# The last part of a four-part transformer kernel: masked keys in place of masked queries, score tiles of 32 rows, three sequences in flight, and keys and values made during the scan

## The chip, the core and the metric

The kernel runs on one core of a Trainium2 chip. Its engines are TensorE (PE in the profile; PEld is its weight load), VectorE (DVE), ScalarE (ACT), GpSimd (POOL) and SyncE (SP, which here only issues transfers). TensorE writes into PSUM, eight banks of 512 float32 per partition; DVE and ACT read PSUM, POOL cannot. The metric is the device time of one launch, in microseconds.

## What is computed

Four attention blocks follow each other on 16 sequences of 256 tokens of width 256. This change touches the end of the third block (a recurrence over the tokens, the scan) and the whole of the fourth:

```python
# third block, its end
def step(s, u_t):
    s = jax.nn.silu(s @ A.T) + u_t
    return (s, s)
_, states = jax.lax.scan(step, jnp.zeros((builder_state.shape[0], S), U.dtype), U.transpose(1, 0, 2))
ssm_out = jnp.einsum('tbs,sh->bth', states, Cmat)
x = residual + ssm_out
# fourth block: dec is x, enc is a context of 77 tokens, 16 heads of 16
q = (dec @ Wq).reshape(b, dec_len, NUM_HEADS, D_HEAD)
kv = enc @ Wkv
kk, v = jnp.split(kv, 2, axis=-1)
attn = jnp.einsum('bihd,bjhd->bijh', q, kk) / jnp.sqrt(jnp.float32(D_HEAD))
attn = jax.nn.softmax(attn, axis=1)
out = jnp.einsum('bijh,bjhd->bihd', attn, v).reshape(b, dec_len, D_INNER)
y = dec + out @ Wfc + bfc
mu = jnp.mean(y, axis=-1, keepdims=True)
var = jnp.mean(jnp.square(y - mu), axis=-1, keepdims=True)
return (y - mu) / jnp.sqrt(var + LN_EPS) * gamma + beta
```

The state has 64 elements per sequence. The softmax of the fourth block runs over the 256 tokens (axis 1), so with the 77 context tokens on the partitions it is a reduction along a row. All matrix products are float32; each such matmul shows as two records in the trace, for every count below.

## The kernel before

The main part (the first two blocks and the third up to the input of the scan, three sequences in flight) is the same in both kernels. Behind it come three stretches.

**Set-up of the scan.** SP issues four transfers: the mean's input, the scan's input `S` (`drive`), the weights of the last part and three rows of parameters. POOL clears some tiles. TensorE then multiplies the input of all tokens (L1670), 32 tokens of all 16 sequences per PSUM bank, eight matmuls of 512 columns into the eight banks. ScalarE waits for all eight.

**The scan.** 254 steps: TensorE multiplies the last state (16 columns) and adds it to its place in PSUM (L1676), ScalarE applies SiLU (L1688), and so on in turn. Nothing else runs. Both engines run it as a loop of two steps with register arithmetic.

**The last part.** For each of 16 sequences `b`: `state` (POOL adds the state and the input, L1762), `dec` (TensorE, L1841, then DVE adds the residual, L1902), `decb` (POOL, L1769), `turn` (four transposes, L1851, evacuated by ACT, L1995), `queries` (L1821, evacuated by ACT, L2004), `keys` (L1821 with 77 columns, ACT L1975) and `values` (L1832, ACT L1987) from a context tile that SP loads (L1747). Then the heads. A score matmul contracts over all 128 partitions, which hold 8 heads of 16, so the other heads must be zero in one operand: POOL's `spread` (L1785) multiplies the queries by a mask, one instruction of 128x256 per head, 16 per sequence. A unit is two heads: one matmul of 512 columns (L1862), DVE's maxima (L1908), ACT's two exponentials with their sums (L2017), DVE's reciprocal of the sums (L1916) and the values scaled by it (L1924). Eight units per sequence. `weigh` (L1872) multiplies weights and values in four 32-column tiles at once, `outputs` (L2026) evacuates, `out` (L1881) projects, then residual (L1933), moments (L1939 to L1945), `rstd` (POOL, L1791), normalise (L1955), gamma and beta (POOL, L1797 and L1802), and the store.

Buffers of the last part exist twice (`TWO = 2`, indexed by `b % TWO`), and so do the statistics of a unit. The order of all steps on each engine is made when the program is built: `plan3()` lists the steps with a cost each and what they wait for, `Plan.order()` lays them out by these costs, and every engine then runs its list strictly in order. A PSUM bank is taken by that plan too. A helper in the main part (L1131) puts matmuls without use into gaps of TensorE; it is not used in the scan or the last part.

## Time and profile before

| | us |
|---|---|
| median of 3 runs | 3063.52 |
| lowest and highest | 3044.8, 3069.33 |
| the profiled execution | 3032.12, span 3030.4 |
| main part, up to 2477 us of the span | 2477.0 |
| set-up of the scan, to 2500.5 | 23.5 |
| scan, to 2730.6 | 230.1 |
| last part, to 3030.4 | 299.8 |

### The profile page before, as it was taken

What the parts mean: (1) busy time and instruction counts of PE and PEld (TensorE: products, weight loads), DVE (VectorE), ACT (ScalarE), POOL (GpSimd) and SP (SyncE); (2) the same over time, 40 slices, a digit from 0 to 9 for tenths busy, and PEclk for the clock granted to TensorE, in tenths of its full rate; (3) what the DMA queues carried; (4) which work ended last, traced back from release to release, by engine and by line L of the source; (5) the groups of instructions that cost most, each with busy time, mean ns of one, the idle gap of its engine ahead of it and who ended that gap; (6) DMA issues with size and microseconds to landing.
All of it is one profiled execution on the core that took longest, in us unless ns stands there. A gap on an engine that the chain in (4) does not pass through costs nothing. (4 is left out here: it accounts for less than half of the span.)

```text
span 3030.4 us, 50406 instructions
## 1 busy us (share of the span) xinstructions
PE 2663.9 (88%) x18092; PEld 1968.6 (65%) x18092; DVE 1787.2 (59%) x4271; ACT 1388.1 (46%) x3588; POOL 878.0 (29%) x1096
## 2 busy tenths in 40 slices
PE   5799999999999999999999999999999974449997
PEld 4577676767676767677777777777767653335443
DVE  3975667666667676667576667575764320005776
ACT  2545455445454554555454454445453312225554
POOL 3540223323232232322232323232321010006676
PEclk9899999999999999999999899999999995559999
DMA  4230101111111111111111111111110010001110
GB/s 190 57 54 3 24 20 34 29 24 34 21 34 27 30 27 27 27 26 28 26 27 26 27 27 30 23 30 23 29 24 10 6 42 0 0 0 38 37 33 23
DMA packets 222419, 90.65 MB, mean 30 GB/s; under 512 B 205280, under 2 KB 212784, under 8 KB 221424
## 3 DMA queue, kind: packets, MB, share of 16 engines
q1 hardware_dynamic: 215728, 67.68, 11.3%
q10 hardware_dynamic: 6464, 19.93, 1.8%
q8 instruction: 144, 2.36, 0.3%
q14 instruction: 83, 0.68, 0.1%
HBM read 27.80 MB, written 9.44 MB: 12 GB/s over the span
## 5 line engine op out<-in xcount | busy, mean ns | idle before, releaser
L1097 PE MATMUL psum<-hT,w_l 128*128 128x256 f32 x2048 | 465.6, 382 | 13.7 <-ACT hT L1433 13.6
L1097 PEld LDWEIGHTS psum<-hT,w_l 128*128 128x128 f32 x2048 | 382.7, 190 | 75.3 <-ACT hT L1433 14.9
L1131 PE MATMUL psum<-w_l 128*128 128x256 f32 x1524 | 382.4, 397 | 7.0 <-ACT work L1557 5.9
L1557 ACT ACTIVATE work<-psum,nbias,qs 128x256 f32<-128x256 f32 x512 | 281.5, 567 | 150.5 <-DVE nbias L1269 147.7
L1131 PEld LDWEIGHTS psum<-w_l 128*128 128x128 f32 x1524 | 287.8, 196 | 67.7 <-issue 18.3
L1573 ACT ACTIVATE work<-psum 128x1024 f32<-128x1024 f32 (+1 forms) x224 | 220.7, 1021 | 241.4 <-PE psum L1029 215.8
L817 POOL TENSOR_TENSOR rstd<-ms,half 128x2 f32<-128x2 f32 (+1 forms) x144 | 101.2, 704 | 629.3 <-DVE ms L1190 483.2
L1266 DVE TENSOR_REDUCE nmax<-psum 128x4 f32<-128x1024 f32 (+1 forms) x192 | 206.5, 1076 | 69.9 <-PE psum L977 69.7
L857 POOL TENSOR_SCALAR work<-work 128x1024 f32<-128x1024 f32 x128 | 136.0, 1062 | 369.2 <-DVE work L1363 345.8
L922 PE MATMUL psum<-hT,w_l 128*128 128x256 f32 x896 | 214.9, 386 | 28.1 <-ACT hT L1433 27.3
L1109 PE MATMUL psum<-w_l,work 128*128 128x256 f32 x1024 | 227.5, 380 | 10.1 <-ACT hT L1433 6.9
L1109 PEld LDWEIGHTS psum<-w_l,work 128*128 128x128 f32 x1024 | 193.3, 190 | 39.7 <-DVE work L1394 12.8
L1676 PE MATMUL psum<-w_l,a_pad 128*64 x508 | 99.3, 275 | 130.6 <-ACT w_l L1688 130.6
L922 PEld LDWEIGHTS psum<-hT,w_l 128*128 128x128 f32 x896 | 163.9, 190 | 62.7 <-issue 25.9
L1285 DVE TENSOR_REDUCE nmp<-psum 128x4 f32<-128x1024 f32 x128 | 148.1, 1218 | 59.6 <-PE psum L991 59.6
L1433 ACT ACTIVATE hT<-psum,cols 128x256 f32<-128x256 f32 x256 | 121.4, 528 | 130.2 <-PE psum L913 129.3
L1363 DVE TENSOR_SCALAR work<-work,rsum 128x256 f32<-128x256 f32 x512 | 176.4, 408 | 4.5
L1676 PEld LDWEIGHTS psum<-w_l,a_pad 128*64 128x64 f32 x508 | 73.4, 206 | 158.0 <-issue 158.0
L931 PE MATMUL psum<-w_l,xhat 128*128 128x256 f32 x640 | 162.3, 398 | 12.6 <-DVE xhat L1342 8.6
L1902 DVE TENSOR_TENSOR w_l<-w_l,psum 128x512 f32<-128x512 f32 x16 | 10.9, 683 | 256.5 <-PE psum L1841 256.4
L2017 ACT ACTIVATE work<-psum,nmax 77x256 f32<-77x256 f32 x256 | 117.6, 464 | 87.8 <-DVE nmax L1908 82.5
L931 PEld LDWEIGHTS psum<-w_l,xhat 128*128 128x128 f32 x640 | 121.7, 197 | 46.0 <-DVE xhat L1342 14.8
(187 smaller groups left out, 4844.2 us busy)
## 6 DMA issues: line engine op xcount, KB each, us to landing
w_l<-in_w_l ACTq DMA_DIRECT2D x1, 5120.0 KB, 25.6
x_res<-in_x SPq DMA_DIRECT2D x16, 256.0 KB, 2.7
res<-x_res ACTq DMA_DIRECT2D x16, 256.0 KB, 3.3
w_l<-res SPq DMA_DIRECT2D x16, 256.0 KB, 2.8
out<-w_l ACTq DMA_DIRECT2D x16, 256.0 KB, 2.0
w_l<-in_w_l ACTq DMA_DIRECT2D x1, 3072.0 KB, 14.0
work<-work SPq DMA_TRANSPOSE x192, 3.1
w_l<-in_w_l SPq DMA_DIRECT2D x2, 1024.0 KB, 8.4
```

Source lines behind the costliest of these rows:

```text
L857: eng.tensor_scalar(e, e, 1.0, MAGIC, ALU.mult, ALU.add).then_inc(*even.next((a.name, u, i, p)))
L922: mm = eng.matmul(banks.tile(key)[:, ft * n:(ft + 1) * n], wt[:, k, ft * P:(ft + 1) * P], src(k), start=(k == 0), stop=(k == KT - 1))
L931: mm = eng.matmul(banks.tile(key)[0:n, m * D:(m + 1) * D], src(k, m), wt[:, k, :], start=(k == 0), stop=(k == KT - 1))
L1097: mm = eng.matmul(banks.tile(key)[:, h * TOKENS:(h + 1) * TOKENS], w1[:, k, h, m * P:(m + 1) * P], hT[p][:, k, :], start=(k == 0), stop=(k ...
L1109: mm = eng.matmul(banks.tile(key)[:, tt * D:(tt + 1) * D], actT(p)[:, m, tt * P:(tt + 1) * P], w2[:, m, :], start=(m == 0), stop=(m == MT ...
L1131: eng.matmul(psum[:, bank, 0:TOKENS], w[0][:, 0:P], w[0][:, 0:TOKENS], start=True, stop=True)
L1266: eng.tensor_reduce(m, s, X, ALU.max, negate=True).then_inc(*norm_step.next(("max", a.name, u, i, p)))
L1285: eng.tensor_reduce(nmp[p][:, half, tile, 64 * i:64 * i + 64:16], s.rearrange("p r (j n) -> p (r j) n", j=2), X, ALU.max, negate=True).the ...
L1363: ins = eng.tensor_scalar(e, e, rsum[:, r, h:h + 1], 255.0, ALU.mult, ALU.min)
L1557: ins = eng.activation(e[:, h * TOKENS:(h + 1) * TOKENS], s[:, h, :], ACT.Exp, bias=nbias[:, r, h:h + 1], scale=qs[:, ATTENTIONS.index(a), ...
L1573: eng.activation(pt(n, p)[0:a.kp, :], banks.pair(key)[0:a.kp, :, :].rearrange("p r n -> p (r n)"), ACT.Exp) \
L1676: eng.matmul(z[0:STATE, n, :], a_pad[:, 0:STATE], G[:, :, n], start=False, stop=True, skip_group_check=True).then_inc(ag_done, 1)
```

## The change

- **Keys are masked, not queries.** For each sequence there are two copies of the keys, one with the even and one with the odd heads kept (`par` is the mask's column, 1 or 0 per partition). A block of 32 partitions holds two heads; a score matmul takes 32 rows of one of the copies, in which one of the two is zero, and the plain queries. POOL's `spread` is gone. A unit is now four heads (`i` picks 64 of the 128 partitions): four matmuls of 32 rows and 256 columns into a pair of banks, two row blocks side by side; one DVE maxima over 77x1024; four exponentials; one reciprocal of four sums; one scaling of 64 elements. Four units per sequence.
- **Three sequences in flight** (`LATE = 3`), three of each buffer, two statistics slots for each.
- **Keys and values are made during the scan.** All 16 context tiles are loaded in the set-up. From step 64 on, every 11 steps, four pieces stand behind a step's matmul: two of the keys (two matmuls of 77 columns each) and two of the values (one of 256 columns). DVE evacuates them in three instructions per sequence.
- **Behind each other step stands a matmul without use** of 208 columns. The scan is written out, without a loop. The eighth input matmul is done before step 33, and ScalarE starts after the first.
- `turn` is evacuated by DVE instead of ACT. The values are scaled as 16 columns per head, with zeros around them, in place of 32. The plan's costs changed, and with them the order.

```diff
-TWO = 2
+LATE = 3
...
+UNITS3 = [(ft, i) for ft in range(KT) for i in range(2)]
...
-        k = add("tensor", "keys", 0, 1.0, *loads, fills=[(("k", b), "scalar", "keys", 0)])
-        v = add("tensor", "values", 0, 0.9, k, fills=[(("v", b), "scalar", "values", 0)])
...
-        slots = [add("pool", "spread", u, 0.9, q, earlier(b, "tensor", "scores", None, 4 + u)) for u in range(4)]
...
+        for u, (ft, i) in enumerate(UNITS3):
+            x = add("tensor", "scores", u, 0.5, q, fills=[(("s", u, b), "scalar", "exps", u)])
+            before = scaled[u - HELD] if u >= HELD else earlier(b, "vector", "scale", None, last)
+            x = add("vector", "maxima", u, 1.25, x, before)
+            x = add("scalar", "exps", u, 2.25, x, earlier(b, "tensor", "weigh", None, ft))
+            scaled.append(add("vector", "scale", u, 0.45, x, *scaled[-1:], earlier(b, "tensor", "weigh", None, ft)))
+            if i:
+                x = add("tensor", "weigh", ft, 0.95, scaled[-1], fills=[(("o", ft, b), "scalar", "outputs", ft)])
+                o.append(add("scalar", "outputs", ft, 0.5, x, earlier(b, "tensor", "out", None, 0)))
...
+        BESIDE = 208
+        BEGIN, EVERY = 2 * CHUNK, 11
...
+                for b in range(BATCH):
+                    eng.dma_start(ctx3[b].rearrange("p k c -> p (k c)"), t["ctxT"][b]).then_inc(kv_in, 16)
...
-                for p in range(TWO):
-                    eng.memset(vpad[p][:, 0, :, :], 0.0).then_inc(blank, 1)
-                eng.wait_ge(blank, TWO)
+                for p in range(LATE):
+                    eng.memset(vs[p], 0.0).then_inc(blank, 1)
+                eng.wait_ge(blank, LATE)
...
+                for b in range(BATCH):
+                    eng.wait_ge(kv_full, b + 1)
+                    for j in range(2):
+                        eng.tensor_scalar(kx3[b][:, j, :, :].rearrange("p f n -> p (f n)"), psum[:, 1, 0:KT * CTX], par[:, j:j + 1], None, ALU.mult)
+                    eng.tensor_copy(v3[b][0:CTX, :], psum[0:CTX, 1, D:2 * D]).then_inc(kv_taken, 1)
...
-                for c in range(TOKENS // CHUNK):
+                last = TOKENS // CHUNK - 1
+                def preload(c):
                     eng.matmul(psum[:, c, :], a_pad[:, :], S[:, :, c * CHUNK:(c + 1) * CHUNK].rearrange("p b t -> p t b"),
                                start=True, stop=True).then_inc(au_done, 1)
+                for c in range(last):
+                    preload(c)
                 eng.wait_ge(zeroed, 2)
...
-                with eng.Fori(0, (TOKENS - 2) // 2) as i:
-                    step(2 * i + 1)
-                    step(2 * i + 2)
+                def idle(bank):
+                    eng.matmul(psum[:, bank, 0:BESIDE], beside[:, 0:P], beside[:, 0:BESIDE], start=True, stop=True)
+                def keys_of(b, ft):
+                    if not b and not ft:
+                        eng.wait_ge(kv_in, 16 * BATCH)
+                        eng.wait_ge(late_in, 32)
+                    if b and not ft:
+                        eng.wait_ge(kv_taken, b)
+                    for k in range(KT):
+                        eng.matmul(psum[:, 1, ft * CTX:(ft + 1) * CTX], wk3[:, k, ft * P:(ft + 1) * P], ctx3[b][:, k, :],
+                                   start=(k == 0), stop=(k == KT - 1))
+                def values_of(b, k):
+                    mm = eng.matmul(psum[0:CTX, 1, D:2 * D], ctx3[b][:, k, :], wv3[:, k, :], start=(k == 0), stop=(k == KT - 1))
+                    if k == KT - 1:
+                        mm.then_inc(kv_full, 1)
+                for n in range(1, TOKENS - 1):
+                    if n == CHUNK + 1:
+                        preload(last)
+                    step(n)
+                    b, piece = divmod(n - BEGIN, EVERY)
+                    if n < BEGIN or b >= BATCH or piece >= 2 * KT:
+                        idle(0 if n > CHUNK else last)
+                    elif piece < KT:
+                        keys_of(b, piece)
+                    else:
+                        values_of(b, piece - KT)
...
-                eng.wait_ge(au_done, TOKENS // CHUNK)
+                eng.wait_ge(au_done, 1)
...
-                with eng.Fori(0, (TOKENS - 2) // 2) as i:
-                    eng.wait_ge(ag_done, 2 * i + 1)
-                    step(2 * i + 1)
-                    eng.wait_ge(ag_done, 2 * i + 2)
-                    step(2 * i + 2)
+                for n in range(1, TOKENS - 1):
+                    eng.wait_ge(ag_done, n)
+                    step(n)
...
-                    for h in (2 * g, 2 * g + 1):
-                        eng.tensor_scalar(kbd3(b)[:, h, :], qT3(b)[:, ft, :], mask16[:, h:h + 1], 1.0, ALU.mult,
-                                          ALU.mult).then_inc(*qbd_ready.next((ft, b, h)))
...
-                    ft, g = units3[u]
+                    ft, i = UNITS3[u]
                     key = ("s", u, b)
-                    ready(key, (qbd_ready, (ft, b, 2 * g + 1)), *([] if u else [(k3_ready, b)]))
-                    eng.matmul(banks3.tile(key)[0:CTX, :], kT3(b)[:, ft, :], kbd3(b)[:, 2 * g:2 * g + 2, :],
-                               start=True, stop=True).then_inc(*banks3.filled(key))
+                    ready(key, *([] if u else [(q3_ready, (b, KT - 1))]))
+                    for j in range(2):
+                        for r in range(2):
+                            g = slice(64 * i + 32 * r, 64 * i + 32 * r + 32)
+                            mm = eng.matmul(banks3.pair(key)[0:CTX, r, j * TOKENS:(j + 1) * TOKENS], kx3[b][g, j, ft, :],
+                                            qT3(b)[g, ft, :], start=True, stop=True)
+                    mm.then_inc(*banks3.filled(key))
...
-                            mm = eng.matmul(banks3.tile(key)[32 * c:32 * c + 32, 0:TOKENS], vs[b][0:CTX, n, :],
+                            mm = eng.matmul(banks3.tile(key)[32 * c:32 * c + 32, 0:TOKENS], vs[b][0:CTX, n, 16 - 16 * h:48 - 16 * h],
                                             pt3(b)[0:CTX, n, :], start=(h == 0), stop=(h == 1))
...
+                def turn(_, n, b):
+                    key = ("decT", b)
+                    eng.wait_ge(*banks3.at(key))
+                    if b >= LATE:
+                        eng.wait_ge(*banks3.at(("q", b - LATE)))
+                    eng.tensor_copy(hT[b % LATE][:, :, :].rearrange("p a b -> p (a b)"), banks3.tile(key)) \
+                        .then_inc(*banks3.released(key, decT_ready, b))
...
-                    key, r = ("s", u, b), b % TWO * TWO + u % TWO
+                    key, r = ("s", u, b), slot3(u, b)
                     eng.wait_ge(*banks3.at(key))
-                    eng.tensor_reduce(nmax[0:CTX, r, 0:2], banks3.tile(key)[0:CTX, :].rearrange("p (h n) -> p h n", h=2),
+                    eng.tensor_reduce(nmax[0:CTX, r, 0:4], banks3.pair(key)[0:CTX].rearrange("p r (j n) -> p (r j) n", j=2),
                                       X, ALU.max, negate=True).then_inc(*max3_ready.next((u, b)))
...
-                    eng.reciprocal(rsum[0:CTX, r, 0:2], sums[0:CTX, r, 0:2]).then_inc(*den3.next((u, b)))
+                    eng.reciprocal(rsum[0:CTX, r, 0:4], sums[0:CTX, r, 0:4]).then_inc(*den3.next((u, b)))
...
-                    eng.tensor_tensor(vs[b][0:CTX, h:h + 2, :], vpad[b % TWO][0:CTX, 0, h:h + 2, :],
-                                      bcast(rsum[0:CTX, r, 0:2].unsqueeze(2), [CTX, 2, 32]), ALU.mult) \
+                    eng.tensor_tensor(vs[b][0:CTX, h:h + 4, 16:32], v3[b][0:CTX, h * 16:h * 16 + 64].rearrange("p (h d) -> p h d", h=4),
+                                      bcast(rsum[0:CTX, r, 0:4].unsqueeze(2), [CTX, 4, 16]), ALU.mult) \
...
-                    for h in range(2):
-                        eng.activation(pt3(b)[0:CTX, ft * 8 + 2 * g + h, :], s_[:, h, :], ACT.Exp,
-                                       bias=nmax[0:CTX, r, h:h + 1], accum_out=sums[0:CTX, r, h:h + 1]) \
-                            .then_inc(*banks3.released(key, exp3_done, (u, b, h)))
+                    s_ = banks3.pair(key)[0:CTX].rearrange("p r (j n) -> p (r j) n", j=2)
+                    for n in range(4):
+                        ins = eng.activation(pt3(b)[0:CTX, h + n, :], s_[:, n, :], ACT.Exp,
+                                             bias=nmax[0:CTX, r, n:n + 1], accum_out=sums[0:CTX, r, n:n + 1])
+                    ins.then_inc(*banks3.released(key, exp3_done, (u, b)))
...
```

What the engines run in the two places that matter, as the program lists it. TensorE from the set-up to the end of the scan, before (w_l is the large tile that holds input and states, a_pad the step's weights; two steps per turn of the loop):

```order
L1670 MATMUL psum<-w_l,a_pad 128x512 x8
L1679 UNCONDITIONAL_BRANCH
L1679 ISA
L1676 ISA
L1676 MATMUL psum<-w_l,a_pad 64x16
```

and in the changed kernel around step 64, where the first sequence's keys and values are made (L1729 is the step, L1734 the matmul without use, L1743 the keys, L1747 the values):

```order
L1729 MATMUL psum<-w_l,a_pad 64x16
L1734 MATMUL psum<-w_l 128x208
L1729 MATMUL psum<-w_l,a_pad 64x16
L1743 MATMUL psum<-w_l 128x77 x2
L1729 MATMUL psum<-w_l,a_pad 64x16
L1743 MATMUL psum<-w_l 128x77 x2
L1729 MATMUL psum<-w_l,a_pad 64x16
L1747 MATMUL psum<-w_l 77x256
L1729 MATMUL psum<-w_l,a_pad 64x16
L1747 MATMUL psum<-w_l 77x256
L1729 MATMUL psum<-w_l,a_pad 64x16
L1734 MATMUL psum<-w_l 128x208
```

So each step's matmul now has one other piece of work behind it in TensorE's queue.

TensorE in the middle of the last part, before (L1841 dec, L1821 keys or queries, L1832 values, L1851 turn, L1872 weigh, L1881 out, L1862 scores):

```order
L1841 MATMUL psum<-cw,w_l 128x256 x2
L1821 MATMUL psum<-w_l 128x77 x4
L1832 MATMUL psum<-w_l 77x256 x2
L1851 MATMUL psum<-ident,w_l 128x128 x4
L1872 MATMUL psum<-work,w_l 32x256 x8
L1821 MATMUL psum<-hT,w_l 128x256 x4
L1881 MATMUL psum<-w_l,xhat 128x256 x4
L1841 MATMUL psum<-cw,w_l 128x256 x2
L1862 MATMUL psum<-work,kcx 77x512 x4
```

and in the changed kernel (L1870 turn, L1895 weigh, L1884 scores, L1904 out, L1851 queries, L1860 dec):

```order
L1870 MATMUL psum<-ident,w_l 128x128 x4
L1895 MATMUL psum<-work,w_l 32x256 x8
L1884 MATMUL psum<-x_res,w_l 77x256 x8
L1904 MATMUL psum<-w_l,xhat 128x256 x4
L1884 MATMUL psum<-x_res,w_l 77x256 x4
L1851 MATMUL psum<-hT,w_l 128x256 x4
L1884 MATMUL psum<-x_res,w_l 77x256 x4
L1860 MATMUL psum<-cw,w_l 128x256 x2
L1884 MATMUL psum<-x_res,w_l 77x256 x4
```

Keys and values are gone, and score units, now four matmuls each, stand singly between steps that use the whole array.

DVE in the same stretch of the changed kernel (L1939 maxima, L1947 and L1953 the scaling, L1925 dec, L1962 residual, then the moments):

```order
L1939 TENSOR_REDUCE nmax<-psum 77x4
L1947 RECIPROCAL rsum<-sums 77x4
L1953 TENSOR_TENSOR w_l<-work,rsum 77x4x16
L1939 TENSOR_REDUCE nmax<-psum 77x4
L1925 TENSOR_TENSOR w_l<-w_l,psum 128x512
L1962 TENSOR_TENSOR w_l<-w_l,psum 128x512
L1968 BN_STATS st<-w_l 128x6 x2
```

Maxima and scalings alternate as before, with half as many of each.

## Rows read from the trace of the kernel before

**Rows 1.** Stretches by stage: us, busy us of PE, PEld, DVE, ACT, POOL, clock, DMA.
```profile
2477.00:2500.50 23.50, 14.12 (x16) 3.66 (x16) 3.97 (x4) 1.32 (x2) 4.50 (x3) 0.74 0.46 120
2500.50:2730.60 230.10, 99.28 (x508) 73.42 (x508) 0.00 (x0) 48.54 (x255) 0.00 (x0) 0.51 0.00 0
2730.60:3030.40 299.80, 266.19 (x1344) 138.92 (x1344) 197.06 (x528) 163.23 (x642) 202.91 (x336) 0.97 0.11 33
```

**Rows 2.** Timeline in the scan: start us, us, engine, line, operation, idle before.
```profile
2501.27 0.19 ACT L1688 ACTIVATE w_l<-psum  x1 [0.62 <-PE psum L1676]
2501.63 0.28 PE L1676 MATMUL psum<-w_l,a_pad 128*64 x2 [0.52 <-ACT w_l L1688]
2502.07 0.19 ACT L1688 ACTIVATE w_l<-psum  x1 [0.61 <-PE psum L1676]
...
2599.87 0.19 ACT L1688 ACTIVATE w_l<-psum  x1 [0.72 <-PE psum L1676]
2600.23 0.39 PE L1676 MATMUL psum<-w_l,a_pad 128*64 x2 [0.52 <-ACT w_l L1688]
2600.78 0.19 ACT L1688 ACTIVATE w_l<-psum  x1 [0.71 <-PE psum L1676]
```

**Rows 3.** Timeline of the main part's end: tiles and whole-array matmuls in turn.
```profile
2386.52 0.70 PE L1131 MATMUL psum<-w_l 128*128 128x256 f32 x2
...
2407.15 1.09 PE L1029 MATMUL psum<-work,kcx 32*77 32x256 f32 x8 [0.54 <-DVE work L1307]
2408.17 1.07 PE L1074 MATMUL psum<-work,vpad 77*32 77x256 f32 x16
2409.17 1.09 PE L1029 MATMUL psum<-work,kcx 32*77 32x256 f32 x8
2410.19 1.13 PE L1131 MATMUL psum<-w_l 128*128 128x256 f32 x4
```

**Rows 4.** Short stretches, two in the main part; columns as in rows 1.
```profile
155.00:160.00 5.00, 3.90 (x35) 2.69 (x34) 4.86 (x11) 0.91 (x3) 3.90 (x5) 1.00 0.00 0
1690.00:1695.00 5.00, 4.48 (x40) 1.68 (x42) 2.91 (x5) 2.61 (x4) 0.00 (x0) 0.50 0.02 3
...
2732.00:2738.00 6.00, 5.08 (x16) 4.13 (x17) 0.69 (x1) 0.30 (x1) 1.49 (x3) 0.50 0.37 111
```

**Rows 5.** The last part's middle, columns as in rows 1.
```profile
2750.00:3000.00 250.00, 231.70 (x1188) 119.41 (x1190) 177.08 (x474) 144.57 (x575) 176.00 (x295) 1.00 0.11 34
```

**Rows 6.** Groups by line in the same 250 us: count, busy us, mean ns, idle before.
```profile
L1908 DVE TENSOR_REDUCE nmax<-psum 77x2 f32<-77x512 f32 x116 | 77.8, 678 | 11.4 <-PE psum L1862 11.2
```

**Rows 7.** Groups by line, the last part: operation, shapes, count, busy us, mean ns, idle.
```profile
L1785 POOL TENSOR_SCALAR work<-x_res,mask 128x256 f32<-128x256 f32 x256 | 120.7, 491 | 54.1 <-ACT x_res L2004 38.8 <-PE psum L1862 10.1 <-PE psum L1841 5.2
L2017 ACT ACTIVATE work<-psum,nmax 77x256 f32<-77x256 f32 x256 | 117.6, 464 | 87.8 <-DVE nmax L1908 82.5 <-POOL w_l L1802 3.1 <-PE psum L1862 2.0
...
L1924 DVE TENSOR_TENSOR w_l<-vpad,rsum 77x64 f32<-77x64 f32 x128 | 51.0, 399 | 7.5 <-ACT vpad L1987 2.8 <-DVE rsum L1916 0.4
L1916 DVE RECIPROCAL rsum<-sums 77x2 f32<-77x2 f32 x128 | 19.7, 154 | 19.9 <-ACT work L2017 19.4
...
L1902 DVE TENSOR_TENSOR w_l<-w_l,psum 128x512 f32<-128x512 f32 x16 | 10.9, 683 | 256.5 <-PE psum L1841 256.4
...
L1987 ACT ACTIVATE vpad<-psum 77x128 f32<-77x128 f32 x32 | 7.0, 277 | 3.5 <-PE psum L1832 3.4
L1975 ACT ACTIVATE kcx<-psum 128x154 f32<-128x154 f32 x16 | 4.7, 293 | 4.5 <-PE psum L1821 4.4
```

**Rows 8.** Line L1285 (maxima, main part): count, min/median/max ns, first and last start.
```profile
L1285 DVE TENSOR_REDUCE nmp<-psum x128: 1187/1217/1228, 225.9 to 2375.6; 128x4 f32<-128x1024 f32 x128
```

**Rows 9.** Timeline of the last part: its beginning (clock 0.50), later, and scores.
```profile
2732.92 1.96 PE L1821 MATMUL psum<-w_l 128*128 128x77 f32 x8 [2.64 <-DMA w_l<-in_ctxT]
...
2741.85 1.01 PE L1821 MATMUL psum<-w_l 128*128 128x77 f32 x8
...
3006.42 3.60 PE L1862 MATMUL psum<-work,kcx 128*77 128x512 f32 x8
```

243 lines of the change are left out of this document (94 added, 149 removed).

## The prediction

> **What bounds the kernel now.** I read the stretches by stage first [rows 1], since the change touches only what lies behind 2477 us of the span: 23.5 us of set-up, 230.1 us of scan, 299.8 us of last part.
>
> The scan is a chain of two engines with no other work. At the full clock, for its first microseconds, one step is 2502.07 - 2501.27 = 0.80 us; at 0.50 it is 2600.78 - 2599.87 = 0.91 us [rows 2]. What differs is TensorE's pair of records, 0.28 against 0.39 us. ScalarE's 0.19 us and TensorE's wait of 0.52 us for it are the same. The granted clock is 0.51 over the scan: TensorE does little, and the chip gives it 1.2 GHz.
>
> The last part is bound by TensorE. In its middle TensorE is busy 231.7 of 250 us, at clock 1.00, DVE 177.1, POOL 176.0, ACT 144.6 [rows 5]. The 116 maxima instructions that start in the middle [rows 6], 8 per sequence, are 14.5 sequences, so a sequence takes 250 / 14.5 = 17.24 us and 15.98 us of TensorE, 12.21 of DVE, 12.14 of POOL, 9.97 of ACT. The last part is then 16 x 17.24 = 275.8 us and 24.0 us for filling and emptying.
>
> **The last part, term by term.** TensorE loses the keys (8 records in 1.01 us [rows 9]; 0.97 without the overlap), the values (two pairs of 256 columns at 0.43, 0.86 [rows 3]) and the old scores: eight records, four units, in 3.60 us [rows 9], of which the last 0.17 lies under what follows, so 0.86 a unit and 6.9 us in all. It gains four units of four 32-row matmuls each. The main part has the same form, L1029 with 32 rows, 77 columns of weights and 256 moving columns, 8 records: it starts 1.02 us before the next step's matmuls, when tiles of another shape follow [rows 3]. So 4 x 1.02 = 4.1 us. A whole-array pair behind tiles takes 0.70 us from its weight load on, 0.27 of it beside the 0.43 that a further pair adds (1.13 for two pairs, the same rows), and starts only when the one before is nearly done; the order shows whole-array steps standing singly between scores, about two more such changes per sequence, 0.15 each: 0.3. TensorE: 15.98 - 0.97 - 0.86 - 6.9 + 4.1 + 0.3 = 11.65 us.
>
> DVE: maxima 4 x 1.217 ([rows 8], there on 128 partitions) for 8 x 0.678; four reciprocals and four scalings fewer, 4 x 0.154 and 4 x 0.399 (64 elements each, as before) [rows 7]; `turn` added, which I price as the other 128x512 from PSUM, 0.683. Together 12.21 - 0.55 - 0.62 - 1.60 + 0.68 = 10.1 us. ACT drops keys 0.29, values 2 x 0.28 and turn, at most about 0.6: 8.5 us. POOL drops 16 x 0.491: 4.3 us. DVE's keys and values work moves under the scan, three instructions per 11 steps, where DVE had nothing to do [rows 1].
>
> So TensorE stays the bound, but DVE is now at 10.1 of 11.65. Before, a sequence took 17.24 / 15.98 = 1.08 of TensorE's work; by that alone it would be 12.6. Three things raise it: DVE, TensorE and ACT wait for each other in strict order within each unit (maxima, four exponentials of 0.464, scaling), with DVE nearly as full as TensorE; a unit is twice as coarse; and tiles may cost clock (below). The other end is the old 17.24. I take 13.3, nearer the lower one, since three sequences in flight give each engine other work during a wait. Filling and emptying stay 24.0, less 3.0: the first keys waited 2.64 us for their transfer [rows 9], and they stand no longer ahead of `dec`. Last part: 16 x 13.3 + 21.0 = 233.8, a gain of 66.0 us.
>
> **The scan, term by term.** Is the matmul without use hidden? At full clock the step's pair lasts 0.28. A next matmul of another shape starts about 0.08 before the last one's end (2407.15 + 1.09 against 2408.17 [rows 3]). The pair of 256 columns takes 0.70; one of 208 columns loses 48/256 of 0.43 us, so 0.62. The next step could start after 0.28 - 0.08 + 0.62 - 0.08 = 0.74 us, and ScalarE lets it start only after 0.80. It is hidden with 0.06 us to spare. Values (256 columns) give 0.82, 32 times 0.02; keys, 4 records some 0.12 us apart (8 in 1.01 [rows 9]), are hidden. The cover is thin: 0.1 us more for any of this and 254 steps cost 10 us. I take 0.82 for a step: 208 us, and 22 us gained.
>
> Does the clock hold? At 155 us TensorE was busy 3.90 of 5 us and kept 1.00; at 1690 it was busy 4.48 of 5 us, with narrow tiles around it, at 0.50 [rows 4]. The new scan is busy most of the time by this count, but with short matmuls, and the key steps stream least. I expect some stretches at half clock, 5 us in all. The written-out input matmul costs in the scan what it saved ahead of it. Sixteen context transfers, 1.3 MB, go out behind the scan's input while the DMA engines are already at a share of 0.46 [rows 1]: I charge 1.5 us. POOL's larger clearing ends well before TensorE's seven input matmuls. Gain of scan and set-up: 22 - 5 - 1.5 = 15.5 us.
>
> The Trainium skill bears on this (TensorEngine Tiling (Array Packing), section Key Properties): changing the tiling mode, not only the tile, drains TensorE. The trace agrees, with the starts a mere 0.08 us before the last end. By that rule every step of the scan drains twice, 64 columns against 128, and the last part at each score unit; both are in the sums above by the rows.
>
> **Sum.** 66.0 + 15.5 = 81.5 us. On the profiled execution, 3032.1 - 81.5 = 2950.6. The median of the three runs lies 31 us above it, in parts that the change does not touch; I carry that over: 3063.5 - 81.5 = 2982.
>
> **The rivals.**
>
> *The last part comes nearer to its bound* (0.18). 12.3 us per sequence and a scan at 0.80 throughout: 82 + 25 = 107 us, 2956. For it: 1.08 was reached before. Against: no engine then had another as full beside it.
>
> *The scan gives nothing* (0.15). The thin cover fails by 0.1 us, or the clock drops at each group of key steps: the scan stays at about 230 us, 3063.5 - 66 + 1.5 = 2999. For it: the 0.06 us, and the drop at 1690 us.
>
> *The last part hardly gains* (0.08). Evacuation binds: DVE's in-order waits for four exponentials at a time hold the maxima of other sequences, and a sequence takes 16.3 us. 3063.5 - 16 x 0.94 - 3 - 15.5 = 3030. For it: the ACT waits for L1908 were 82.5 us of the last part [rows 7]. Against: that was with TensorE as the bound. The Trainium skill warns of this (the same page, section PSUM Bottleneck): tiling speeds TensorE up but not the evacuation of PSUM, which may become the bound. The rows' 10.1 us for DVE leaves room.
>
> *Slower: the clock stays at 1.2 GHz through the scan* (0.07). Then the added matmul is a cost. Its time doubles as the narrow matmuls' did, 1.96 against 1.01 us [rows 9]: 0.62 becomes about 1.05 with its fixed part, a step 0.39 - 0.08 + 1.05 - 0.08 = 1.28 us, 254 of them 325 us, 95 more than now. With the last part's gain: 3063.5 - 66 + 95 = 3093. It decides from about 0.26 us per step on (66 / 254). Against it: TensorE comes from 12 us of full work when the scan starts, at 0.99 and above in the first steps, and keeps far busier than in the old scan; at 1.05 of 1.28 us it is busier still. The Trainium skill (TensorE: Matmul & The Clock Gate, Part 1) has it that the idle state is the throttled one and activity releases it, which is on the side of a scan that recovers; how much activity these short pairs are is for the run to tell.
>
> **How the numbers follow.** The forecast has 0.52: 2982, its own range 2960 to 3000, from 12.6 to 14.3 us per sequence and 0 to 22 us from the scan. The range for 8 in 10 takes in the better last part and the lost scan and ends before the weak last part and the slow clock: 2940 to 3030. The lower end also holds a median that falls nearer to the profiled execution. About 1% (31 us) is what a measurement of this kernel can tell from no change. Faster by over 1%: forecast, first two rivals and a little of the third, 0.87. Within 1%: the rest of the third and slow clock in part of the scan, 0.07. Slower: 0.06.
>
> **What would show it.** In the changed profile: scan steps at 0.80 to 0.83 us with the granted clock at 1.00, about 208 us from first to last SiLU, with a few slices below; a step whose matmul starts right behind the useless one's end, with no wait for ScalarE, says the cover is gone. In the last part, about 234 us: TensorE busy 85 to 90% at 1.00, score units 1.0 us apart from what follows, maxima 1.2 us each, DVE busy about 10 us per sequence, POOL a third. DVE above 90% would make it the bound; a clock below 0.95 there would say that the tiles cost clock, which my 13.3 holds only in part. Set-up of 22 to 26 us. The main part unchanged. I am wrong if the scan's clock is 0.5 or the time per sequence is outside 12.3 to 14.5 us.

## The result, and the profile after

| | us |
|---|---|
| before, median of 4 runs | 3055.61 (3044.8 to 3069.33) |
| after, median of 4 runs | 2960.64 (2954.39 to 2969.67) |
| ratio | 0.9689, 95% interval 0.9636 to 0.9742 |
| the profiled execution | 2969.67, span 2967.9 |

The change makes the kernel 95 us (3.1%) faster; 82 us were forecast.

Stretches by stage, profile of the changed kernel (us, busy us of PE, PEld, DVE, ACT and POOL with counts, granted clock, DMA share, GB/s). The lines are set-up of the scan, scan, last part, and the middle of the last part. They answer to [rows 1] and [rows 5].

```profile
2502.10:2523.40 21.30, 12.36 (x15) 3.44 (x15) 4.36 (x4) 1.47 (x2) 5.60 (x4) 0.69 0.73 192
2523.40:2722.60 199.20, 199.20 (x1083) 128.83 (x1082) 15.82 (x48) 48.58 (x254) 0.00 (x0) 1.00 0.00 1
2722.60:2967.90 245.30, 207.88 (x1410) 124.66 (x1408) 171.54 (x352) 140.98 (x577) 82.60 (x80) 0.83 0.11 35
2740.00:2940.00 200.00, 179.84 (x1219) 107.34 (x1218) 148.22 (x300) 123.60 (x511) 65.04 (x62) 0.83 0.09 31
```

Set-up and scan fell from 253.6 to 220.5 us, the last part from 299.8 to 245.3. That is 33.1 + 54.5 = 87.6 us. The scan holds the full clock throughout. The last part now runs at 0.83 instead of 0.97.

The main part takes 2502.1 us here and 2477.0 in the profile of before, with the same code. It varies from execution to execution with the time spent at half clock. Over all 14 profiles of this case the last matmul of the main part starts at 2470.0 to 2503.8 us, with 109 to 212 us of half clock ahead of it, and the short ones are those with little of it. So I compare profiles by what lies **behind the main part**, from the start of that last matmul to the end of the span: 557.4 us before, 470.1 after, 87.3 us less.

Timeline in the scan, the same profile, weight loads left out (start us, us, engine, line, operation, count, idle before). First plain steps with the matmul without use (L1734), then the first steps with keys (L1743) and values (L1747). They answer to [rows 2].

```profile
2524.13 0.29 PE L1729 MATMUL psum<-w_l,a_pad 128*64 128x16 f32 x2
2524.35 0.62 PE L1734 MATMUL psum<-w_l 128*128 128x208 f32 x2
2524.46 0.19 ACT L1769 ACTIVATE w_l<-psum 64x16 f32<-64x16 f32 x1 [0.57 <-PE psum L1729]
2524.90 0.29 PE L1729 MATMUL psum<-w_l,a_pad 128*64 128x16 f32 x2
...
2573.66 0.67 PE L1743 MATMUL psum<-w_l 128*128 128x77 f32 x4
2573.76 0.19 ACT L1769 ACTIVATE w_l<-psum 64x16 f32<-64x16 f32 x1 [0.57 <-PE psum L1729]
2574.26 0.29 PE L1729 MATMUL psum<-w_l,a_pad 128*64 128x16 f32 x2
...
2575.29 0.66 PE L1747 MATMUL psum<-w_l 128*77 128x256 f32 x2
2575.40 0.19 ACT L1769 ACTIVATE w_l<-psum 64x16 f32<-64x16 f32 x1 [0.63 <-PE psum L1729]
2575.88 0.29 PE L1729 MATMUL psum<-w_l,a_pad 128*64 128x16 f32 x2
```

A plain step is 0.77 us, one with keys 0.82, one with values 0.81. ScalarE ends at 2524.46 + 0.19 = 2524.65, yet the next step's matmul starts at 2524.90, right behind the matmul without use. By the sign that the prediction named, the cover is gone.

Groups by line in the same 200 us of the last part (count, busy us, mean ns, idle before). They answer to [rows 6] and [rows 7].

```profile
L2017 ACT ACTIVATE work<-psum,nmax 77x256 f32<-77x256 f32 x228 | 104.0, 472 | 26.2 <-DVE nmax L1939 25.9
L1939 DVE TENSOR_REDUCE nmax<-psum 77x4 f32<-77x1024 f32 x57 | 68.7, 1213 | 19.1 <-PE psum L1884 19.0
```

57 maxima, four per sequence, are 14.25 sequences. A sequence takes 200 / 14.25 = 14.04 us, with 12.62 us of TensorE, 10.40 of DVE, 8.67 of ACT and 4.56 of POOL. Filling and emptying are 245.3 - 16 x 14.04 = 20.7 us.

### The profile page after: what moved, and what is told of

The parts are those of the page before. It is cut to its first block and busy times, and to the rows that moved or that the text cites. A ratio compares the mean times of both kernels' runs of the same rounds, so it can differ in the third digit from the quotient of the medians.

```text
span 2967.9 us, 49392 instructions
## 1 busy us (share of the span) xinstructions
PE 2727.7 (92%) x18728; PEld 2023.1 (68%) x18728; DVE 1779.4 (60%) x4143; ACT 1367.0 (46%) x3524; POOL 758.7 (26%) x841
## 3 DMA queue, kind: packets, MB, share of 16 engines
q1 hardware_dynamic: 215728, 67.68, 11.5%
## 5 line engine op out<-in xcount | busy, mean ns | idle before, releaser
L1127 PE MATMUL psum<-w_l 128*128 128x256 f32 x1524 | 392.6, 405 | 7.0 <-ACT work L1553 5.9
L1105 PE MATMUL psum<-w_l,work 128*128 128x256 f32 x1024 | 227.5, 380 | 10.1 <-ACT hT L1429 6.9
L1376 DVE TENSOR_TENSOR x_res<-x_res,psum 128x512 f32<-128x512 f32 x112 | 76.6, 684 | 122.9 <-PE psum L927 63.9
L857 POOL TENSOR_SCALAR work<-work 128x1024 bf16<-128x1024 f32 x128 | 134.0, 1047 | 10.6
L1586 ACT ACTIVATE work<-psum,cols 128x256 f32<-128x256 f32 x128 | 60.3, 474 | 162.8 <-PE psum L1093 162.5
```

The costliest lines, as they stand in the source:

```text
L857: eng.tensor_scalar(rounded_part(a, u, i, p), e, -MAGIC, 1.0, ALU.add, ALU.mult) \
L1105: mm = eng.matmul(banks.tile(key)[:, tt * D:(tt + 1) * D], actT(p)[:, m, tt * P:(tt + 1) * P], w2[:, m, :], start=(m == 0), stop=(m == MT ...
L1127: eng.matmul(psum[:, bank, 0:TOKENS], w[0][:, 0:P], w[0][:, 0:TOKENS], start=True, stop=True)
```

## Experiments on the scan

**The loops of the kernel before written out, nothing else** (before, ScalarE's side alike):

```diff
-                with eng.Fori(0, (TOKENS - 2) // 2) as i:
-                    step(2 * i + 1)
-                    step(2 * i + 2)
+                for n in range(1, TOKENS - 1):
+                    step(n)
```

> The kernel before with the two loops of the scan written out and nothing else changed. Theory A: the clock stays at 0.50 and a step goes from 0.91 to about 0.88 us: 5 to 10 us less. Rival B: the loop's own instructions were the whole difference between 0.91 and 0.77: some 30 us less.

Measured: 2989.5 us against 3051.5, ratio 0.9801 (0.9758 to 0.9844); 497.8 us behind the main part against 557.4. Timeline in its scan, at half clock:

```profile
2600.16 0.19 ACT L1687 ACTIVATE w_l<-psum 64x16 f32<-64x16 f32 x1 [0.48 <-PE psum L1676]
2600.40 0.29 PEld L1676 LDWEIGHTS psum<-w_l,a_pad 128*64 128x64 f32 x2 [0.39 <-ACT w_l L1687]
2600.40 0.39 PE L1676 MATMUL psum<-w_l,a_pad 128*64 128x16 f32 x2 [0.28 <-ACT w_l L1687]
2600.83 0.19 ACT L1687 ACTIVATE w_l<-psum 64x16 f32<-64x16 f32 x1 [0.48 <-PE psum L1676]
```

Its first steps are still at the full clock, 0.57 us apart:

```profile
2520.34 0.19 ACT L1687 ACTIVATE w_l<-psum 64x16 f32<-64x16 f32 x1 [0.38 <-PE psum L1676]
...
2520.91 0.19 ACT L1687 ACTIVATE w_l<-psum 64x16 f32<-64x16 f32 x1 [0.38 <-PE psum L1676]
```

A step at half clock takes 0.67 us in place of 0.91 with the clock, TensorE's pair (0.39) and ScalarE's 0.19 as they were. Both ways between the engines got shorter. From ScalarE's end to the next matmul: 2600.40 - 2600.35 = 0.05 us, before 0.17 (2600.23 - 2600.06, [rows 2]). From the matmul's start to ScalarE's: 0.43, before 0.55. So 2 x 0.12 us of each step belonged to the loop. I had named 0.03; both theories were too low, and the gain of 62 us is twice what the rival gave. The last part is as before, 299.6 us at 0.97.

The trace of before held a sign of it that I had not asked for: the groups by line over the scan, weight loads, first before and then this kernel.

```profile
L1676 PEld LDWEIGHTS psum<-w_l,a_pad 128*64 128x64 f32 x508 | 73.4, 206 | 158.0 <-issue 158.0
```

```profile
L1676 PEld LDWEIGHTS psum<-w_l,a_pad 128*64 128x64 f32 x508 | 72.3, 202 | 99.8 <-ACT w_l L1687 97.8 <-issue 2.0
```

```profile
L1676 PEldq FUSED_REGOPS  x254: 74/74/78, 2500.7 to 2729.8; - x127
L1688 ACTq FUSED_REGOPS  x254: 74/74/83, 2501.1 to 2730.3; - x127
L1679 PEldq COMPARE_BRANCH  x127: 76/208/235, 2501.8 to 2730.0; - x127
```

In the loop the wait stands in a register instruction ahead of the load, and ahead of the activation on ScalarE; written out, it stands on the load and the activation themselves. In the trace of before the load starts 0.124 us after its register instruction does, the activation 0.121 us (medians of 250 steps). Those instructions start 0.037 us behind ScalarE's end and 0.427 behind the matmul's start, where the written-out scan has the load 0.051 and the activation 0.430 behind (medians too). So the 0.12 us of each crossing come with the register instruction that holds the wait. The branch is not on the way: it comes at every second step, and steps with and without it both take 0.907 us. The Trainium skill (Runtime: NRT & Kernel Launch, Instruction fetch mechanics) warns of branches for another reason, a fetch stall, and says that kernels prefer full unrolling. The equal steps show no such stall here.

**The same with the matmul without use** (in place of nothing behind the step, with the eighth input matmul at step 33 and ScalarE starting after the first):

```diff
+                    if n == CHUNK + 1:
+                        preload(last)
                     step(n)
+                    eng.matmul(psum[:, 0 if n > CHUNK else last, 0:208], S[:, 0, 0:P], S[:, 0, 0:208], start=True, stop=True)
```

> The kernel before with the scan alone changed: written out, the eighth input matmul at step 33, ScalarE starting after the first, and a matmul without use of 208 columns behind every step; no keys and values there. Theory: clock 1.00 in the scan, 0.77 us per step, 198 us in place of 230 and set-up some 1 us shorter: 30 to 34 us less than the kernel before (3055.6 to about 3023), a ratio of 0.990, and the rest of the 95 us gain of the change then belongs to the last part (about 60). Rival: the scan gains only together with keys and values, or gives back what it gains to the last part by a lower clock there: less than 20 us.

Measured: 3006.9 us against 3051.5, ratio 0.9857 (0.9825 to 0.9889), 522.3 us behind the main part. Stretches, scan and last part:

```profile
2493.00:2692.50 199.50, 199.50 (x1021) 124.80 (x1020) 0.00 (x0) 48.56 (x254) 0.00 (x0) 1.00 0.00 1
2692.50:2992.30 299.80, 266.01 (x1346) 138.43 (x1345) 197.15 (x528) 163.53 (x642) 203.61 (x336) 0.97 0.11 33
```

The steps are 0.77 us at clock 1.00, and the last part is 299.8 us at 0.97 as before, so the scan gives nothing back there. The 35.1 us gained behind the main part are just above the 30 to 34 expected, and they are 24.5 us less than the bare steps gained. The matmul without use brings the full clock, which is worth 0.10 us per step (0.57 against 0.67, below), and costs 0.20.

**The changed kernel without it**, keys and values staying between the steps:

```diff
-                        idle(0 if n > CHUNK else last)
+                        pass
```

> The changed kernel without the matmuls without use in the scan; keys and values stay between the steps. Theory A (these matmuls hold the clock, and that is most of the scan's gain): the granted clock falls to about 0.50 for the scan, a plain step takes 0.88 us (0.91 of the kernel before, less 0.03 for the written-out loop) against 0.77, and the 64 steps with keys or values take 1.1 to 1.3 us, since their matmuls then double too; the scan goes from 199 to 225 to 250 us and the time up by 25 to 50 us. Rival B (the written-out loop is the gain): the scan stays within 8 us of 199.

Measured: 2983.8 us, ratio 0.9768 (0.9734 to 0.9802), 487.0 us behind the main part, 16.9 more than the changed kernel. That is less than the 25 to 50 us of theory A, and more than the 8 us of rival B. Timeline, a plain step and one with keys:

```profile
2575.77 0.19 ACT L1769 ACTIVATE w_l<-psum 64x16 f32<-64x16 f32 x1 [0.48 <-PE psum L1729]
...
2576.34 1.14 PE L1743 MATMUL psum<-w_l 128*128 128x77 f32 x4
2576.45 0.19 ACT L1769 ACTIVATE w_l<-psum 64x16 f32<-64x16 f32 x1 [0.48 <-PE psum L1729]
2577.41 0.29 PEld L1729 LDWEIGHTS psum<-w_l,a_pad 128*64 128x64 f32 x2
2577.41 0.40 PE L1729 MATMUL psum<-w_l,a_pad 128*64 128x16 f32 x2
```

The clock falls as theory A has it, but its times were off both ways. Some 186 plain steps then take 0.67 us (0.88 expected), less than the 0.77 with the matmul without use, and 64 steps with keys or values take 1.39 (1.1 to 1.3 expected), more than the 0.81. The whole loss is theirs: 64 x 0.58 = 37 us against 19 us won on the plain ones. So in the changed kernel the matmul without use pays only through the keys and values beside it.

**Widths.** Two ladders on the kernel before with the written-out scan, one up and one down, one execution each. The first:

```diff
+                    width = 16 + 48 * ((n - 1) // 51)
```

> The kernel before with the written-out scan and matmuls without use, whose width changes every 51 steps: 16, 64, 112, 160 and 208 columns. Theory: the matmul without use is not hidden, it sets the step: with the loop gone ScalarE and TensorE alone need 0.57 us at full clock (the four such steps of the written-out scan without any) and 0.67 at half clock, and a step with w columns takes the larger of 0.57 and 0.22 us + the pair's time - 0.08, where the pair takes 0.62 at 208 columns and 0.0017 us less per column: 0.57, 0.57, 0.60, 0.68 and 0.77 us, if the clock stays at 1.00. Where the clock falls to 0.50 (most likely at 16 columns), 0.67 or more. Rival: 0.77 us is a floor that ScalarE and the semaphores set at full clock: 0.77 for all widths.

The second:

```diff
+                    width = (176, 144, 112, 80, 48, 16)[(n - 1) // 43]
```

> The kernel before with the written-out scan and matmuls without use whose width falls along the scan: 176, 144, 112, 80, 48 and 16 columns, 43 steps each. It starts at the full clock with work enough to hold it. Theory: at the full clock a step takes the larger of 0.57 us and 0.22 us + the pair - 0.08, so 0.71, 0.65, 0.60, 0.57 and 0.57 us; from some width on, 112 columns or fewer, the clock falls and does not come back in the scan, as it did not in the ladder that began at 16 columns; from there on a step takes that ladder's half-clock times, 1.03 us at 112, about 0.98 at 80, 0.92 at 48 and 0.87 at 16. Rival: the clock depends on the number of matmuls and not on their width, and falls at no width or at the start of the scan (1.2 us per step at 176 columns).

Us per step, from ScalarE's starts:

| columns | 16 | 48 | 64 | 80 | 112 | 144 | 160 | 176 | 208 |
|---|---|---|---|---|---|---|---|---|---|
| full clock | 0.57 | | | | 0.62 | 0.66 | | 0.71 | 0.77 |
| half clock | 0.87 | 0.92 | 0.95 | 0.97 | 1.03 | | 1.16 | | 1.32 |

The full clock's 208 is the changed kernel's; 16 and 112 held it for three steps each. The step follows the width, so 0.77 is no floor of ScalarE, and the theory's 0.60, 0.65 and 0.71 came as 0.62, 0.66 and 0.71. The first ladder lost the clock at 16 columns and never had it back: 280 us for its scan, 596.2 behind the main part. The second, which began with 176, kept it down to 144 and lost it three steps into the 112. Stretches of the second (144 columns, then 112 behind the fall) and of the first (208 columns, its last 54 us):

```profile
2551.00:2578.00 27.00, 27.00 (x165) 19.96 (x164) 0.00 (x0) 7.85 (x41) 0.00 (x0) 1.00 0.00 1
2583.00:2617.00 34.00, 34.00 (x134) 26.25 (x133) 0.00 (x0) 6.31 (x33) 0.00 (x0) 0.50 0.00 0
```

```profile
2730.00:2784.00 54.00, 54.00 (x165) 32.40 (x165) 0.00 (x0) 7.83 (x41) 0.00 (x0) 0.50 0.00 0
```

The same work, a step and 208 columns, ran at 1.00 for 199.5 us in the scan with the matmul without use (above), which began it at the full clock, and at 0.50 for all of its 54 us here, where it began at half clock. So in these runs the clock that this work began with stayed; whether it would return after more than 54 us, no run shows. TensorE's records cover 54.0 of 54.0 us, so a busy share of 100% did not bring the clock back in that time. The Trainium skill (TensorE: Matmul & The Clock Gate, Part 1) says that activity releases the throttle; by busy records this stretch does not agree.

**144 columns in the changed kernel:**

```diff
-        BESIDE = 208
+        BESIDE = 144
```

> The changed kernel with one number changed: the matmul without use has 144 columns instead of 208. Theory: it sets the step, so a plain step falls from 0.77 to 0.66 us at the full clock, which 144 columns held in the falling ladder; 190 plain steps save 0.11 us each, the 64 with keys or values stay at 0.81: 209 us of scan go to about 188, and the time from 2960.6 to about 2940. Rival: the clock falls at the steps with keys or values, where TensorE streams least, and does not come back: 190 steps at 1.1 us and 64 at 1.39, some 80 us slower.

Ten executions gave 2970.2 to 3038.6 us, seven of them above 3027, with a median of 3031.0; two of 9.5 and 11.8 ms, unexplained, are left out. The ratio that was formed, 0.982 (0.9776 to 0.9864), counts only the three lowest and flatters it: the quickest had a mean clock of 0.943, the other nine 0.916 to 0.930. Behind the main part, in the profiled execution of 3035.3 us: 538.3 us, 68 more than with 208. The rival was right. Timeline at the second group of keys and values, part of its lines:

```profile
2573.28 0.67 PE L1743 MATMUL psum<-w_l 128*128 128x77 f32 x4
...
2574.09 1.11 PE L1747 MATMUL psum<-w_l 128*77 128x256 f32 x2
...
2575.47 1.14 PE L1747 MATMUL psum<-w_l 128*77 128x256 f32 x2
...
2578.74 0.29 PEld L1729 LDWEIGHTS psum<-w_l,a_pad 128*64 128x64 f32 x2 [0.28 <-issue]
2578.75 0.40 PE L1729 MATMUL psum<-w_l,a_pad 128*64 128x16 f32 x2
2579.07 0.85 PE L1734 MATMUL psum<-w_l 128*128 128x144 f32 x2
```

The clock falls between the keys and the values of that group. From there to the last step a plain step takes 1.11 us, where 0.66 had been reached. In the scan of the run with the plan's measured costs (last below), the same code, it fell some 40 steps later. The five profiled scans with 208 columns from their start kept 1.00 to their end. So the step from 144 to 208 columns is a margin that the profile of the change doesn't show by itself.

## Experiments on the last part

**Keys and values back in the last part, the scan written out and bare.** The core of the edit (DVE evacuates them there, and SP loads three context tiles in turn):

```diff
+        k = add("tensor", "keys", 0, 1.0, earlier(b, "tensor", "scores", None, last), fills=[(("k", b), "vector", "keys", 0)])
+        v = add("tensor", "values", 0, 0.9, k, fills=[(("v", b), "vector", "values", 0)])
+        k = add("vector", "keys", 0, 0.66, k)
+        v = add("vector", "values", 0, 0.41, v)
...
-                        idle(0 if n > CHUNK else last)
-                    elif piece < KT:
-                        keys_of(b, piece)
-                    else:
-                        values_of(b, piece - KT)
```

> The changed kernel with the scan written out and bare (no matmul without use, no keys or values), and keys and values made in the last part again, evacuated by DVE, from three context tiles loaded there. Theory: the bare scan takes 0.67 us per step at half clock, 171 us in place of 209 with its set-up 10 us later: 26 to 30 us less; keys and values cost the last part TensorE 1.83 us and DVE 1.07 us per sequence, 2.0 us in all at 1.11 times TensorE's work, 245 to about 277 us. Sum: about 2 to 6 us slower than the changed kernel. Rival: DVE, not TensorE, is what fills the last part: 1.07 us per sequence, 17 us, and the kernel is 10 us faster.

Measured: 2945.7 us, ratio 0.9654 (0.9595 to 0.9713), 455.8 us behind the main part. (One of its four executions, 3472 us, and one of 3907 us in the kernel with late keys and added matmuls below, are as far off and as unexplained as the two above.) Stretches, scan and last part:

```profile
2512.00:2685.00 173.00, 102.18 (x511) 72.84 (x510) 0.00 (x0) 48.38 (x254) 0.00 (x0) 0.51 0.00 0
2685.00:2942.60 257.60, 218.52 (x1600) 142.32 (x1600) 187.38 (x400) 141.71 (x578) 83.15 (x80) 0.88 0.13 39
```

The scan is as expected. Keys and values cost the last part 257.6 - 245.3 = 12.3 us and not 32. They did not go into TensorE's gaps, which are 257.6 - 218.5 = 39.1 us here and were 245.3 - 207.9 = 37.4. TensorE's busy time rose by only 10.6 us, though its matmuls for keys and values are busy 38.4 us (19.3 + 19.1): those of all its other lines sum to 193.9 us here and 216.4 in the changed kernel. The clock is 0.88 here against 0.83; how much of this is the clock and how much the new order, no run separates. The theory of 2 to 6 us slower failed. The rival's numbers (17 us, 10 us faster) came nearer, its reason did not: DVE is busy 187.4 of 257.6 us, 73%. Behind the main part this kernel is 14.3 us shorter than the changed one. Its ratio's interval overlaps that of the change, so it is the better one by the profiles and likely by the times. Its scan also doesn't depend on a clock that must not fall.

**Matmuls without use in the last part**, 59 of them, between narrow steps (scores, weigh) that follow each other:

```diff
+            if t[1] in ("scores", "weigh") and narrow:
+                when, bank = min((self.end[takers[last[b]]] + HOP if last[b] else 0.0, b) for b in range(8))
+                if when <= self.end[t] - self.us[t]:
+                    self.idle[t] = bank, last[bank], 1
+            narrow = t[1] in ("scores", "weigh")
```

> The changed kernel with 59 matmuls without use (256 columns, 0.43 us each, 25 us of TensorE) in the last part, one in front of a narrow step (scores or weigh) that stands right behind another narrow step. Theory: the clock falls in the last part where only narrow steps follow each other, so these hold it at 0.97 or above against 0.83; TensorE then has 11.6 + 1.6 = 13.2 us per sequence against the 12.6 seen, and the time stays within 8 us of the changed kernel, since the clock gives back what the added work costs. Rival 1: the clock's dips cost the last part 10 us or more (14.04 us per sequence against the forecast 13.3): then the last part falls below 237 us all the same. Rival 2: the tiles are not the cause and the clock stays below 0.90: 10 to 25 us slower.

Stretches, last part and its middle:

```profile
2726.70:2964.00 237.30, 219.91 (x1528) 128.32 (x1527) 171.41 (x352) 140.55 (x578) 82.68 (x80) 0.99 0.11 36
2744.00:2944.00 200.00, 195.03 (x1369) 113.35 (x1370) 154.55 (x318) 127.09 (x526) 66.38 (x64) 1.00 0.09 31
```

Groups by line in that middle:

```profile
L1962 DVE TENSOR_REDUCE nmax<-psum 77x4 f32<-77x1024 f32 x59 | 71.6, 1215 | 17.8 <-PE psum L1901 17.6
```

The clock is held. 59 maxima are 14.75 sequences: 13.56 us each in place of 14.04, though TensorE has 13.22 us of work in them. (A count of maxima is good to about 0.25 us per sequence; the whole last part gives the same difference, 8.0 / 16 = 0.50.) The last part is 8.0 us shorter than in the changed kernel; at 237.3 us it just misses the first rival's 237. The time, 2968.7 us with a ratio of 0.9722 (0.9692 to 0.9752), doesn't show it; it is not lower than that of the change. So holding the clock is worth about 8 us of the last part by the profile, net of the added matmuls' own time, and this is no cure that the times confirm. That narrow steps in a row bring the fall is supported, not proven: the added matmuls stand just there, and the clock stayed.

The same addition in the kernel with late keys and values:

> A kernel put together from what the runs showed: the scan written out and bare (0.67 us per step at half clock), keys and values in the last part, and 46 matmuls without use there between narrow steps that follow each other. Theory: scan 182 us and the last part at a clock of 0.97 or above, 5 to 10 us shorter than the 257.8 without them: 2935 to 2942 in all, 20 to 25 us faster than the changed kernel. Rival: TensorE is fuller here (keys and values add 1.8 us per sequence), and the added matmuls cost what the clock gives: 2945 us as without them, or some us more.

Measured: 2959.0 us, ratio 0.9688 (0.9648 to 0.9729), 13 us more than without. Stretch, last part:

```profile
2688.30:2955.70 267.40, 246.12 (x1692) 152.10 (x1692) 187.37 (x400) 142.08 (x578) 83.43 (x80) 0.95 0.13 37
```

The last part went from 257.6 to 267.4 us with the clock at 0.95, and it is the rival's side that came true. Why added matmuls shorten the changed kernel's last part by 8.0 us and lengthen this one by 9.8 is open. A fuller TensorE alone doesn't tell them apart: it is busy 246.1 of 267.4 us here, 92%, and was busy 219.9 of 237.3 there, 93%. The clock had less to give back here (0.88 to 0.95 against 0.83 to 0.99).

**Two sequences in flight in the plan** (one line, `earlier` in `plan3()`):

```diff
-        return (*task, b - LATE) if b >= LATE else None
+        return (*task, b - 2) if b >= 2 else None
```

> The changed kernel with an order for the last part that lets two sequences be in flight instead of three (the buffers stay three). Theory: TensorE waits for DVE and ACT more often, and the last part goes from 245 to 255 to 270 us; the plan itself is 9 us longer. Rival: two were enough (the last part stays within 5 us), and the third sequence had no part in the gain.

**`turn` evacuated by ACT:**

```diff
-        x = add("vector", "turn", 0, 0.7, x, earlier(b, "tensor", "queries", None, 0))
+        x = add("scalar", "turn", 0, 0.6, x, earlier(b, "tensor", "queries", None, 0))
```

> The changed kernel with the turned tokens evacuated by ACT (about 0.6 us) instead of DVE (0.68 us), as before. Theory: DVE with 10.4 of 14.04 us per sequence is not the bound and ACT (8.7) has to serve four exponentials in a row, so the move gains nothing and may cost: the last part 243 to 258 us (the plan is 28 us longer by its own costs). Rival: DVE is the bound beside TensorE: the last part gets 5 to 11 us shorter.

The last part of each (one execution each), two in flight and then `turn` on ACT:

```profile
2714.50:2977.60 263.10, 212.80 (x1410) 129.18 (x1409) 175.83 (x352) 142.14 (x578) 82.47 (x80) 0.80 0.10 33
```

```profile
2711.10:2987.30 276.20, 220.01 (x1410) 130.13 (x1408) 171.24 (x336) 149.94 (x593) 82.74 (x80) 0.81 0.09 31
```

Two in flight cost 17.8 us, within what was expected. `turn` on ACT costs 30.9 us, more than the 13 that I allowed, while its plan is 28 us longer by its own costs. The move changes the whole order with it, so how much is ACT's load and how much the order stays open. For the same reason this run can't settle whether DVE binds; against it speaks that DVE is busy 10.40 of 14.04 us in the changed kernel.

Of the last part's 54.5 us, then, 12.3 go with the keys and values and 17.8 with the third sequence in flight, each taken alone. The rest is the new form of the scores, POOL's `spread` gone, `turn` on DVE and the order together. No run puts the old score units back, so the share of the masked keys, the change's first item, is not measured by itself.

**Costs in the plan as measured**, for the last part, on the 144 columns:

```diff
-            x = add("tensor", "scores", u, 0.5, q, fills=[(("s", u, b), "scalar", "exps", u)])
+            x = add("tensor", "scores", u, 1.02, q, fills=[(("s", u, b), "scalar", "exps", u)])
```

> The kernel of the run with 144 columns, with the plan's costs for the last part set to what the trace shows: dec 1.06, turn 0.55, queries 1.93, scores 1.02, weigh 1.0, out 1.93, the exponentials 1.9 us; nothing else. Theory: the plan now counts 11.55 us of TensorE per sequence instead of 8.75, its order leaves fewer waits, and the last part goes from 245 to 235 to 242 us; its bound by clock dips stays. Rival: the order is not what costs the last part, and it stays within 4 us of 245, or gets longer.

The last part is 251.6 us at clock 0.83, 5 to 6 us longer than with the change's costs (245.3 and 246.6 with 144 columns). The expected 235 to 242 failed and the rival was right: true costs don't give a better order here. The time (3023.8 us) is that of the scan that lost its clock.

## The prediction, point by point

- **The last part, term by term: the work was right, the time per sequence 0.7 us too low.** Score units start 1.02 us apart as taken from the main part (2778.73 - 2777.71), queries and `out` take 1.93 us, `dec` 1.07, `turn` about 0.6, `weigh` 1.0 twice: 1.93 x 2 + 1.07 + 0.6 + 2.0 + 4 x 1.02 = 11.6 us of TensorE at full clock, forecast 11.65. DVE has 10.40 (10.1), ACT 8.67 (8.5), POOL 4.56 (4.3), a maxima 1213 ns (1217), and filling and emptying 20.7 (21.0). Timeline of TensorE in the last part:

```profile
2777.71 1.09 PE L1884 MATMUL psum<-x_res,w_l 32*77 32x256 f32 x8
2778.73 1.99 PE L1851 MATMUL psum<-hT,w_l 128*128 128x256 f32 x8
...
2818.09 1.07 PE L1895 MATMUL psum<-work,w_l 77*32 77x256 f32 x16 [1.72 <-DVE hT L1933]
2819.09 2.75 PE L1884 MATMUL psum<-x_res,vpad 32*77 32x256 f32 x16
2821.77 3.78 PE L1904 MATMUL psum<-w_l,xhat 128*128 128x256 f32 x8
```

- **What raised 13.3 to 14.04 was named, but not sized.** "A clock below 0.95 there would say that the tiles cost clock, which my 13.3 holds only in part": it is 0.83. At the end of the lines above, two units of scores for 2.75 us instead of 2 x 1.02 and an `out` for 3.78 instead of 1.99 run at half clock, behind a stretch with nothing but narrow steps and a wait. With the clock held a sequence took 13.56 us. So about 0.5 of the 0.74 us are the clock, net of the added matmuls; the rest no run takes apart. The term that was mis-sized is the last part's 66.0, measured 54.5.
- **The scan: the forecast sum was 17.6 us too low, and its central step failed.** "It is hidden with 0.06 us to spare" (0.74 against 0.80) compared the new work to the chain of the loop. I had read that chain as ScalarE, semaphores and TensorE, and carried it over to a scan without a loop, though the diff shows that the loop goes. Its own chain is 0.57 us at full clock and 0.67 at half. The 0.74 was nearly right (0.77 measured). It just is the bound and not the cover.
- **The reason for the gain failed with it.** I put the scan's gain on the clock (0.91 to 0.80). Bare written-out steps at half clock give 59.6 us behind the main part; with the added matmuls and the full clock the gain is 35.1. The clock is worth 0.10 us per step and its price is 0.20. What the forecast had at nothing is the loop: 0.24 us per step.
- **Clock in the scan:** 5 us of dips were allowed, none came. The rival of a scan that stays at 1.2 GHz, 1.28 us per step, didn't happen at 208 columns, but its mechanism is real: 1.32 us per step in the ladder, 1.11 with 144 columns. What the prediction had against it (a scan entered at the full clock) fits the runs with 208 columns, and did not save the scan with 144.
- **Set-up:** 21.3 us against 23.5; the sixteen context tiles cost no time that the stages show, and no wait for them is seen in the scan.
- **Sum and carry-over.** 66.0 + 15.5 = 81.5 forecast, 54.5 + 33.1 = 87.6 measured, out of two errors of opposite sign (-11.5, +17.6). That the sum came out near is luck: the scan's gain came from the loop, which the forecast had at nothing. The profile of before was a quick one of its kind, 23.5 us below the later median, so that carrying 31 us over was about 8 too much. The forecast of 2982 is 21 us above the measured median: 8 from there, 6 from the stages, and the rest from the medians, which lie 95.0 us apart where the stages of the two profiles differ by 87.6. The measured time lies in the range, in the likeliest case's own range by 0.6 us only.

## What to carry to other kernels

Before work is put into the gaps of a chain between two engines, measure the chain in the form that it will have: written out, without a loop. Where a loop's waits stand in register instructions, each crossing pays for them (0.12 us here); a weight load whose idle time ends in "issue" is a hint to look, though that time holds the wait itself too. Removing the loop gave more (62 us for a few lines) than the scan with the matmul without use (45 us). Work that is added to hold TensorE's clock must be priced against its own length per step, and tried from half clock too, since the same work ran at 1.00 for 199.5 us and at 0.50 for 54.

## What the runs showed of the hardware

- A loop with register arithmetic cost 0.12 us at each of the two crossings between TensorE and ScalarE, 0.24 of a step of 0.91 us. The register instruction that holds the wait takes 74 ns, and the work behind it starts 0.12 us after its start. The branch, at every second step, cost nothing: both kinds of step take 0.907 us.
- The granted clock stayed at 0.50 for the last 268 us of the first ladder's scan, 2517 to 2785 us, while TensorE's records left no gap, at 0.87 to 1.32 us per step. The same 208 columns per step begun at 1.00 stayed at 1.00 for 199.5 us. In the ladder it returned 8.5 us into the last part, at 2793.5 us, behind whole-array matmuls of 77 and 256 columns.
- 144 columns behind each step held the clock for 43 steps where nothing else stood between, and lost it in both profiled scans with keys and values between, some 40 steps apart in the same code.
- The same main part took 34 us more or less, with 109 to 212 us of it at half clock.
